# Another order for the first FFN, the q/k/v projections and the first four maxima of a hybrid block

## The reference

```python
x = x + mixer(_layernorm(x))
x = x + ffn(_layernorm(x))
x = x + attention(_layernorm(x))
x = x + ffn(_layernorm(x))

def ffn(x):                       # 128 -> 512 -> 128, weights made ternary and scaled
    h = _bitlinear(x, w_fc) + gate * (x @ v.T @ fast_b.T @ u.T)
    r = jnp.maximum(h, 0.0)
    return _bitlinear(r * r, w_proj)

def attention(x):
    qkv = x @ qkv_w.T + qkv_b     # 16 heads, 8 wide
    ...
    w = jax.nn.softmax(q^T k / sqrt(8))     # needs the maximum of each row of scores
    return (w v) @ out_w.T + out_b
```

## Time and profile before

| quantity | value |
| --- | --- |
| median of 3 runs | 534.73 us (534.6 to 534.86) |
| the profiled execution's own time | 534.02 us |
| its span in the trace | 532.0 us |
| PE busy | 499.4 us (94%) |
| DVE busy | 443.0 us (83%) |
| ACT busy | 352.0 us (66%) |

### The profile page before, as it was taken

The page is one execution under the profiler, slowest core; times in us unless marked ns, Lnnn a source line. Parts: engine busy times, 40 slices in busy tenths (PEclk is TensorE's granted clock), DMA queues, the critical chain, the costliest instruction groups (busy, mean ns, idle before and its releaser), DMA issues.

```text
span 532.0 us, 10257 instructions
## 1 busy us (share of the span) xinstructions
PE 499.4 (94%) x4110; PEld 228.9 (43%) x4110; DVE 443.0 (83%) x666; ACT 352.0 (66%) x679; POOL 69.7 (13%) x89
## 2 busy tenths in 40 slices
PE   3999998997899999999999999999999999998797
PEld 2454565774333333333333333333333333333476
DVE  5699249877997999999999999999999999912853
ACT  2736213343005888988888888888888888898431
POOL 4399930000010001001001000000000000000000
PEclk9999999999556999999999999999999999999999
DMA  8100000045300112002001101100200000000001
GB/s 213 36 2 2 1 9 1 1 174 196 106 1 1 42 42 75 9 1 61 24 1 47 38 2 35 48 2 22 62 2 2 2 2 3 1 1 2 0 21 60
DMA packets 14109, 17.96 MB, mean 34 GB/s; under 512 B 3599, under 2 KB 10174, under 8 KB 13550
## 3 DMA queue, kind: packets, MB, share of 16 engines
q1 hardware_dynamic: 13036, 16.58, 10.5%
q0 software_dynamic: 240, 0.46, 0.4%
q10 hardware_dynamic: 786, 0.27, 0.2%
HBM read 11.70 MB, written 5.24 MB: 32 GB/s over the span
## 4 chain that ended last, share of the span: by engine, by line
PE 82%; DVE 10%; ACT 4%; issue 1%; DMA 1%; SPq 0%; ACTq 0%
PE ps L1298 30%; PE ps L1349 26%; PE ps L1073 7%; PE ps L1083 6%; DVE mx L977 4%; PE ps L1316 2%; PE ps L1094 2%; DVE h L761 2%; PE ps L1119 1%; ACT gate L707 1%; PE ps L1105 1%; PE ps L1130 1%; DVE x L869 1%; PE ps L1060 1%; DVE st L738 1%
## 5 line engine op out<-in xcount | busy, mean ns | idle before, releaser
L977 DVE TENSOR_REDUCE mx<-ps 128x1 f32<-128x1024 f32 x256 | 311.7, 1224 | 14.8 <-PE ps L1298 11.6
L1298 PE MATMUL ps<-kt,qt 62*128 62x512 f32 x512 | 197.2, 469 | 6.3 <-DVE mx L977 4.7
L1316 PE MATMUL ps<-qt,kt 64*128 64x512 f32 x512 | 182.5, 450 | 1.4 <-ACT gate L707 1.3
L707 ACT ACTIVATE acc<-ps 128x512 f32<-128x512 f32 x256 | 138.3, 603 | 24.7 <-PE ps L1316 19.7
L707 ACT ACTIVATE gate<-ps 128x512 f32<-128x512 f32 x256 | 138.0, 603 | 15.2 <-PE ps L1316 9.9
L1298 PEld LDWEIGHTS ps<-kt,qt 62*128 62x128 f32 x512 | 81.4, 196 | 111.4 <-DVE mx L977 81.9
L1349 PE MATMUL ps<-gate,val 128*32 128x256 f32 (+1 forms) x976 | 81.2, 405 | 3.8 <-ACT gate L707 3.8
L1316 PEld LDWEIGHTS ps<-qt,kt 64*128 64x128 f32 x512 | 75.7, 186 | 12.7 <-ACT gate L707 5.4
L1349 PE MATMUL ps<-acc,val 128*32 128x256 f32 (+1 forms) x968 | 80.3, 403 | 0.9 <-ACT acc L707 0.9
L493 POOL TENSOR_TENSOR nm_s<-nm,nm_s 16x128 f32<-16x128 f32 x16 | 7.1, 447 | 266.8 <-ACTq L685 266.8
L1349 PEld LDWEIGHTS ps<-gate,val 128*32 128x32 f32 x976 | 19.3, 108 | 46.8 <-issue 24.8
(11 more groups left out here) (179 smaller groups left out, 362.2 us busy)
## 6 DMA issues: line engine op xcount, KB each, us to landing
qt<-q_scr SPq DMA_DIRECT2D x64, 64.0 KB
kt<-k_scr SPq DMA_DIRECT2D x32, 128.0 KB
x<-in_L_attn_a_x SPq DMA_DIRECT2D x4, 256.0 KB, 5.3
q_scr<-attn SPq DMA_DIRECT2D x4, 256.0 KB, 2.2
k_scr<-attn SPq DMA_DIRECT2D x4, 256.0 KB, 2.6
q_scr<-gate SPq DMA_DIRECT2D x4, 256.0 KB, 2.3
k_scr<-gate SPq DMA_DIRECT2D x4, 256.0 KB, 2.6
qt<-nm_s SPq DMA_DIRECT2D x64, 4.0 KB
```

What stands on the lines that cost most here:

```text
L707: act.activation(pexp[step % NPB][:, j, :], bank(e_bank(slot)), ACT.Exp, scale=SCALE).then_inc(e_read, 1)
L977: dve.tensor_reduce(mx[:, item % 2, at:at + 1], pair(lo), AX.X, ALU.max).then_inc(m_read, 1)
L1298: mm = pe.matmul(bank(m_banks(M_UNIT[u])[keys]), qt[r][rows, half, jj, c * P:(c + 1) * P], kt[r][rows, jj, keys, :], start=True, stop=True)
L1316: pe.matmul(bank(e_bank(slot)), kt[r][rows, jj, s // TC, s % TC * P:(s % TC + 1) * P], qt[r][rows, half, jj, :], start=True, stop=True).th ...
```

## The change

It writes another order on three engines, and gives some results other PSUM banks so that the order can be kept.

```diff
@@ PE @@
-            fc(0, TURN_F1, WIDE_F1)
-            turn_h(1, TURN_F1 + 1)
-            turn_h(1, TURN_F1 + 2)
-            fc(1, TURN_F1, WIDE_F1)
-            proj(0, 0, TOK_F1)
-            turn_h(1, TURN_F1 + 3)
-            fc(2, TURN_F1, WIDE_F1)
-            proj(1, 0, TOK_F1)
-            turn_h(2, TURN_QKV)
-            fc(3, TURN_F1, WIDE_F1)
-            turn_h(2, TURN_QKV + 1)
-            qk(0)
-            v(0)
-            qk(1)
-            v(1)
...
+            fc(0, TURN_F1, WIDE_F1)
+            turn_h(1, TURN_F1 + 1)
+            fc(1, TURN_F1, WIDE_F1)
+            turn_h(1, TURN_F1 + 2)
+            turn_h(1, TURN_F1 + 3)
+            proj(0, 0, TOK_F1)
+            proj(1, 0, TOK_F1)
+            fc(2, TURN_F1, WIDE_F1)
+            turn_h(2, TURN_QKV)
+            turn_h(2, TURN_QKV + 1)
+            qk(0)
+            qk(1)
+            v(0)
+            v(1)
+            pe.wait_ge(qk_read, 4)
+            fc(3, TURN_F1, WIDE_F1)
+            proj(2, 0, TOK_F1)
+            proj(3, 0, TOK_F1)
+            turn_h(2, TURN_QKV + 2)
+            pe.wait_ge(tok_read, TOK_F1[2] + 1)
+            unit(0)
+            unit(1)
+            qk(2)
+            v(2)
+            unit(2)
+            turn_h(2, TURN_QKV + 3)
+            unit(3)
+            qk(3)
+            v(3)
@@ DVE @@
-            squares(0, WIDE_F1, TOK_F1)
-            norm(1, 3)
-            for c in range(NCH):
-                if c + 1 < NCH:
-                    squares(c + 1, WIDE_F1, TOK_F1)
-                if c == 2:
-                    qkv_out(0)
-                    qkv_out(1)
-                take_tokens(TOK_F1, c)
-                dve.wait_ge(tok_read, TOK_F1[c] + 1)
-                chunk_stats(2, c)
-                norm(2, c)
-            qkv_out(2)
-            qkv_out(3)
+            squares(0, WIDE_F1, TOK_F1)
+            norm(1, 3)
+            squares(1, WIDE_F1, TOK_F1)
+            take_normed(0)
+            take_normed(1)
+            squares(2, WIDE_F1, TOK_F1)
+            qkv_out(0)
+            qkv_out(1)
+            squares(3, WIDE_F1, TOK_F1)
+            take_normed(2)
+            unit_max(0)
+            take_normed(3)
+            unit_max(1)
+            qkv_out(2)
+            unit_max(2)
+            unit_max(3)
+            qkv_out(3)
+            for u in range(AMONG, NU):
@@ ACT @@
             rectify(0, WIDE_F1, 0)
-            turn_copy(TURN_F1 + 2)
             stds(1, 3)
             rectify(1, WIDE_F1, 0)
+            turn_copy(TURN_F1 + 2)
             turn_copy(TURN_F1 + 3)
             stds(2, 0)
+            stds(2, 1)
             rectify(2, WIDE_F1, 0)
             turn_copy(TURN_QKV)
-            stds(2, 1)
-            rectify(3, WIDE_F1, 0)
             turn_copy(TURN_QKV + 1)
             first_parts(0)
             first_parts(1)
+            rectify(3, WIDE_F1, 0)
@@ banks and waits @@
+AMONG = 4
+QK_BANKS = ((2, 3), (4, 5), (2, 3), (2, 3))
+def turn_bank(i):
+    return 0 if i == TURN_QKV + NCH - 1 else i % 2
+def tok_bank(i):
+    return 1 if i in (TOK_F1[3], TOK_V[2], TOK_V[3]) else 6 + i % 2
@@ qk(c) on PE @@
+                pe.wait_ge(wide_read, WIDE_F1 + KH * (3 if c < 2 else 4))
+                if c == 3:
+                    pe.wait_ge(qk_read, 2 * c)
@@ tokens(i) on PE @@
-                    pe.wait_ge(tok_read, i - 1)
+                    pe.wait_ge(tok_read, i if tok_bank(i) == tok_bank(i - 1) else i - 1)
```

More of the change, by code:

```diff
@@ L293, in build @@
         part0_ready = sem("part0_ready")
+        qk_mm, qk_read = sem("qk_mm"), sem("qk_read")
         scr_done = [sem(f"scr_done{i}") for i in range(2)]
@@ L524, in turn_copy @@
                 act.wait_ge(turn_mm, i + 1)
-                act.activation(hT[:, c * CH:(c + 1) * CH], bank(i % 2), ACT.Copy).then_inc(turned, 1)
+                act.activation(hT[:, c * CH:(c + 1) * CH], bank(turn_bank(i)), ACT.Copy).then_inc(turned, 1)
             def ev(k, dst, src, func=ACT.Copy, **kw):
@@ L633, in first_parts @@
                 for w in range(2):
-                    i = WIDE_QK + 2 * c + w
-                    act.wait_ge(wide_mm, i + 1)
+                    act.wait_ge(qk_mm, 2 * c + w + 1)
                     if c >= 2:
                         act.wait_ge(scr_done[c % 2], STORED * (c // 2))
-                    act.activation(qk_s[c % 2][:, w, 0, :].bitcast(F32R), bank(2 + i % 4), ACT.Identity,
+                    act.activation(qk_s[c % 2][:, w, 0, :].bitcast(F32R), bank(QK_BANKS[c][w]), ACT.Identity,
                                    bias=ob_T[:, ROW_B + BQ + w:ROW_B + BQ + w + 1]).then_inc(part0_ready, 1)
@@ L926, in qkv_out @@
                 for w in range(2):
[L927 removed]
                     dve.wait_ge(part0_ready, 2 * c + w + 1)
[L929 removed]
+                    dve.scalar_tensor_tensor(out=qk_s[c % 2][:, w, 1, :].bitcast(F32R), in0=bank(QK_BANKS[c][w]),
                                              scalar=ob_T[:, ROW_B + BQ + w:ROW_B + BQ + w + 1], in1=qk_s[c % 2][:, w, 0, :],
[L931 removed]
+                                             op0=ALU.add, op1=ALU.subtract).then_inc(qk_read, 1)
                 dve.wait_ge(tok_mm, TOK_V[c] + 1)
[L933 removed]
+                dve.tensor_tensor(v_tok[:, tiles, :], bank(tok_bank(TOK_V[c])).rearrange("p (i d) -> p i d", d=D),
                                   bv_bc[:, :].unsqueeze(1).broadcast_to([P, TC, D]), ALU.add).then_inc(tok_read, 1)
@@ L1003, in projected, with take_normed @@
                 chunk_stats(3, c)
-            for u in range(NU):
+            def take_normed(c):
+                take_tokens(TOK_F1, c)
+                dve.wait_ge(tok_read, TOK_F1[c] + 1)
+                chunk_stats(2, c)
+                norm(2, c)
+            squares(0, WIDE_F1, TOK_F1)
[16 more added lines that the diff above has]
+            for u in range(AMONG, NU):
                 n, at = divmod(u, 2 * HT)
@@ L1249, in qk @@
                 pe.wait_ge(turned, TURN_QKV + c + 1)
+                pe.wait_ge(wide_read, WIDE_F1 + KH * (3 if c < 2 else 4))
+                if c == 3:
+                    pe.wait_ge(qk_read, 2 * c)
                 for w in range(2):
-                    wide(WIDE_QK + 2 * c + w, [(att_T[:, w, :], hT[:, c * CH:(c + 1) * CH])])
+                    pe.matmul(bank(QK_BANKS[c][w]), att_T[:, w, :], hT[:, c * CH:(c + 1) * CH],
+                              start=True, stop=True).then_inc(qk_mm, 1)
             def v(c):
@@ L1301, in max_mm, with unit, loads @@
                     mm.then_inc(m_mm, 1)
+            def unit(u):
+                max_unit(u)
+                max_mm(u, 0)
+                max_mm(u, 1)
+            def loads(n):
+                return (n // NBUF + 1) * LOADS + 32
+            fc(0, TURN_F1, WIDE_F1)
[27 more added lines that the diff above has]
+            v(3)
             def e_free(slot):
@@ L1362, in project @@
                 tokens(TOK_AO[c], lambda t: [(h[:, TC * c + t, :], att_T[:, 3, :])])
[L1364 to L1367, removed]
+            for u in range(AMONG, HT + LEAD):
                 if u == HT + TURN_MAX_AT:
+                    pe.wait_ge(qk_read, 2 * NCH)
+                    pe.wait_ge(tok_read, TOK_V[-1] + 1)
                     turn_max(0)
-                max_unit(u)
-                max_mm(u, 0)
-                max_mm(u, 1)
+                unit(u)
             for hn in range(NI):
```

21 lines of the change are left out of this document (5 added, 16 removed).

## The result

The changed kernel takes 538.35 us (median of 5 runs, 538.05 to 540.87), the kernel before 534.73 us (5 runs, 534.16 to 535.28). The ratio is 1.0077, with a 95% interval from 1.0053 to 1.0101: slower by 3.6 us at the medians.

A forecast was written before the change was run, and what follows sets the result against it. DVE was taken to set the run of maxima, with PE at half clock. 3.9 us lost ahead of chunk 2's addition and 1.3 won behind it make 2.6 late: 534.73 + 2.6 = 537.4 us, range 535.2 to 539.3.

The forecast's parts named there:

- (a): Addition of chunk 0 on DVE: `proj(0)` now stands behind the turn of chunk 3, so it starts 1.44 us late.
- (b): DVE after `proj(0)`: `take_normed(0)` and `take_normed(1)` in a row, 3.93 us each, ending at 106.68.
- (c): Start of q and k of the first batch: `qk(0)` at about 108.5 instead of 109.38, 0.9 us earlier.
- (d): Ahead of chunk 2's addition: `fc(3)` waits for DVE's read of k and joins the chain; addition 3.9 us late.
- (e): From chunk 2's addition to maximum 4: 1.3 us won back, maximum 4 at 140.45 against 137.83, 2.6 us late.
- (f): Loads of the first group: landed no later than before, by about 126.4, so unit 0 at 126.8 waits for nothing; cost nothing.
- The clock: PE's clock ahead of `qk(3)`: it may fall in a thin stretch, but the forecast kept the full rate for `qk(3)`.
- the early fall: Rival: clock falls before `qk(3)`, slowing it and `v(3)`, 1.45 us more, 538.9 us; chance 0.25.
- The rival with a full clock: Clock stays full through the maxima, each of 20 taking 1.24 us; 0.65 late, 535.4 us; chance 0.10.
- The maxima fill waits, if the first part keeps its time: Rival: chunk 2's addition still starts at 118.38, so all 1.3 us behind it is won, 533.4 us; chance 0.08.

The follow-up runs named there:

- The two undone edits: Two separate runs against the changed kernel: `fc(3)` back ahead of `qk(0)`, 538.43 us; `proj(0)` ahead of the turn of chunk 3, 538.22 us.
- another run of these steps, One kernel: Changed kernel plus six spare products behind unit 2 and three behind each of units 6 to 21: 4 runs at 534.8 to 535.6 us, 8 at 545.0 to 548.5.
- the run with the maxima alone: Kernel before with its old order up to the turn of chunk 2, then units 0 to 3 between the steps of chunks 2 and 3: 536.57 us.
- The run with a full clock: Kernel before with two maxima moved behind v(2), six spare products behind unit 3 and three behind each of units 4 to 21: 529.40 us.
- the kernel with six more behind unit 5: Changed kernel with six spare products behind unit 2, three behind each of units 6 to 21, and six more behind unit 5: median 538.72 us.
- the first part alone: Changed kernel with no maximum between the last chunks, all 24 units behind v(3), only the first part's new order left: 539.06 us, ratio 1.0073.

## Why the prediction came out right, and where it was off

I forecast 537.4 us, in a range of 535.2 to 539.3, with 0.82 on slower. Measured is 538.35.

- **(a) `proj(0)` behind the turn of chunk 3, 1.44 late.** Measured 1.52. The run with `proj(0)` first gets 1.00 of it back at the addition of chunk 2. Shown.
- **(b) two `take_normed` in a row.** 104.02 less 100.09 is 3.93, as taken.
- **(c) q and k start earlier.** `qk(0)` starts at +23.95 against +24.66 before, 0.7 earlier (0.9 forecast); the wait of PE ahead of it is 1.12.
- **(d) `fc(3)` in the chain behind the read of k, 3.9 late at the addition of chunk 2.** Measured 4.29, with the waits where they were expected: 1.31, 1.13 and 1.25 on DVE (1.2 each forecast), 1.21 on PE (1.4 forecast). The two undone edits give back 3.44 and 1.00. The 0.4 beyond the forecast is hand-offs of about 0.1 each that the sum had rounded off.
- **(e) behind it, 1.3 won.** Measured 4.29 - 3.76 = 0.5. This is the term with the largest error, and in it are two that worked against each other. A maximum with its scores ready takes 1.13 to 1.15 us, not 1.24 (129.28 to 130.43 in the changed kernel), which with smaller overlaps makes 0.5 less over these steps. And the clock fell in `qk(3)`, which cost the 0.95 us wait for the first part of k, where the sum had DVE wait for unit 0 only; with the clock full in another run of these steps, the stretch was 1.05 shorter. Unit 0 came 0.17 later. And maximum 4 of before, which I had put at 137.83 with 1.24 a maximum, was at 137.67.
- **(f) loads in time.** The outcome held, with more room than I saw: loads landed by 126.4 and unit 0 at 126.8 were 0.4 us. In the run with the maxima alone PE's wait for `kt<-k_scr` ends at 127.13, 10.46 us after DVE's last read of k of chunk 1 at 116.67. With `fc(3)` ahead of `qk(0)` the same step takes 10.51 (127.13 less 116.62). In the changed kernel that last read ends at 116.50, so k should land at 126.96, 1.6 us ahead of unit 0; that is an estimate, since there nothing waits for it. The DMA share that I read the earlier trace rows tells when the last byte comes, and q's other half, which unit 0 does not need, comes behind k.
- **The clock.** Of the rivals the early fall is the one that happened, in part: it fell within `qk(3)` and was back by `v(3)`, which took 1.18 us and not 1.78, so its price was 1.0 and not 1.45. Forecast plus this is 538.4, but that this meets 538.35 so closely is luck: 0.4 too little in (d), 0.3 in the start of unit 0 and maximum 4 of before, and 0.5 too much for the maxima cancel almost. I had given it 0.25 by an argument that fits, a thin stretch ahead of `qk(3)`, and should have given it more. The rival with a full clock I priced wrongly: I took 0.03 us a unit from 1.268 - 1.24, but the 1.24 already held the wait for PE. The run with a full clock shows 1.137, so half clock costs 0.13 a unit, 2.9 us over 22 units. What it costs at the loop's start, which I put at 1.45, no run shows: in the kernels with spare products the clock is down there too. In the trace of the kernel with six more behind unit 5, where the clock was full from maximum 4 to the loop, the last addition is 0.56 us later than before the change. That is near the 0.65 of this rival by luck: maximum 4 is 3.65 us late there, not 2.6, and the maxima win 2.75, not 0.5.
- **The maxima fill waits, if the first part keeps its time.** True with two of them behind v(2) and false with four ahead of it: there the load is late.

The mechanism is the forecast one: the waits ahead of the addition of chunk 2, where the changed kernel loses its time, are those of the sum, the two edits undone give the loss back, and the loop behind is a plain shift (391.07 us from maximum 4 to the last addition against 391.06). What failed is the size of (e), and with it the gain that the maxima were to bring: 2.6 us late were forecast, 3.6 are measured.

What stays open: why one of the five runs of the changed kernel (540.87), two of six of the first part alone (542.0 and 542.1) and two of ten with six spare products (541.5 and 542.6) are 2.5 to 4.3 us longer than their medians. Their mean clocks are low (0.959 to 0.965), though shorter runs have such clocks too, and the one trace that has a fall during `qk(0)` and `qk(1)` shows a cost of 1.7 us from it; that these runs have the same fall is argued, not shown. Open too is why the clock falls in `qk(3)` in some runs and not in others with the same instructions ahead of it.

## What to carry to other kernels

Before an operation is moved ahead on one engine, write down what it leaves behind: `fc(3)` was hidden under DVE's work ahead of q and k, and behind them it was a part of the chain, 3.4 us for a start of q that was 0.7 earlier. A stage that reads data back from DRAM has a time before which nothing of it may stand in an in-order queue; place work from the landing of the load, not from the first wait that looks free. And where two engines alternate on double buffers, the time of one operation read there holds its wait for the other; take it from a place where its input lies ready.

## What the runs showed of the hardware

- **PE's clock fell behind thin stretches, and spare products could hold it.** The Trainium skill, page "TensorE: Matmul & The Clock Gate", section "What's actually happening", says that activity releases the throttle; the traces agree. In the kernel with two maxima moved PE was busy for 0.39 of 2.00 us from 133 to 135, and the clock fell from 2.4 to 1.2 GHz between 137 and 139 us. With spare products (1.66 of 2.00 us in the same place, three a unit behind it) it stayed full through the run of maxima and fell once they had ended.
- **It is not the same in every run.** One kernel had 4 runs of 12 near 535 us and 8 at 545 us and more, 9 to 14 us apart. The trace of one of the eight shows why: at half clock the spare products themselves set the pace, 3.41 us for two units. Two spare products a unit neither held the clock nor cost anything (532.73 against 532.54 us).
- **f32 products of 128x512 take 1.8 to 1.9 times as long at half clock:** the two of `qk(3)` took 3.57 us in the changed kernel, where the clock fell just after their start, and 3.75 with `proj(0)` first, where it was down all the while (0.50 from 136 to 139 us), against 1.98 for `qk(2)`.
- **DVE reductions of 128x1024 from PSUM start 1.13 to 1.14 us apart** although each is recorded with 1.22 to 1.24: neighbours overlap by 0.1 us when no wait stands between them.
